# A graph-network kernel in which VectorE's running minimum is moved ahead of a step's first left-over columns

## The chip, the cores and the metric

One core of a Trainium2 chip runs the whole program. The metric is the device time of one execution in microseconds (us), lower being better.

## What is computed

The reference takes 6250 nodes with 64 features and 206250 edges sorted by destination, normalises the nodes, and runs four layers. In a layer each edge carries a message, and each node needs the sum, mean, variance, greatest and least of the messages that reach it; these feed a dense update with two batch norms.

```python
msg = jnp.concatenate([h[src], h[dst]], axis=1) @ WM + bM
s = jax.ops.segment_sum(msg, dst, num_segments=n)
mean_sq = jax.ops.segment_sum(msg * msg, dst, num_segments=n) / denom
mx = jnp.where(has, jax.ops.segment_max(msg, dst, num_segments=n), 0.0)
mn = jnp.where(has, jax.ops.segment_min(msg, dst, num_segments=n), 0.0)
agg = jnp.concatenate([mean, mx, mn, std, var, s], axis=1)
```

The part of a message that depends on the destination is added after the aggregation, so what is gathered or multiplied per edge is one row of a table of 6250 source nodes (the projected features and their squares).

## The kernel before

The kernel meets the segment sums and extremes in two ways at once, in what is called the dense phase of a layer below.

**One way is dense.** The 6250 destinations, in an order of their own, are cut into 13 chunks of 482 (`NCH`, `CH`); the sources into 50 blocks of 125 (`TILES`). For one edge per destination and block, TensorE multiplies the block's table (split in three bf16 parts) by a one-hot matrix. `products` (L1791) picks, for four blocks at a time, the source row of each destination into a pair of PSUM banks; a destination without an edge there gets a hugely negative number. `sums` (L1817) adds the rows of all blocks. In its middle it calls `flips` (L1800), which turns the hugely negative numbers in the same banks into hugely positive ones. VectorE folds the banks into running results: `greatest` (L1363, the first step of a chunk L1361) before the flip, `least_of` (L1374, the first L1372) after it. Three such pairs of banks are used in turn (`QRING`). A step is four blocks; a chunk has 13 steps, of which the last has two blocks, so a layer has 169 steps. TensorE's order in a step is products(i), first half of sums(i-1), flips(i-1), second half of sums(i-1). flips(i) waits for greatest(i), least_of(i) waits for flips(i), and products(i+3) waits for least_of(i).

**The other way is by columns.** Edges that are second, third and so on within one block for their destination are "left over". They are listed in 457 columns of 128 rows; GpSimd issues one indirect DMA for each (L883), which gathers 128 table rows into `rows`, and ScalarE masks what was gathered (L634). The columns come in 166 groups of one to three. VectorE treats a group twice, in `column_group`: part 0 folds greatest and least (L1435, L1436), part 1, six blocks later, adds the sums (L1440). The gathers go into a ring of five groups (`RING_G`): GpSimd may not issue the gathers of group g+5 before part 1 of group g has signalled `joined`.

**The order on VectorE** is written out. `columns_at` gives each half of a step (two blocks) the parts due there. Within step i VectorE runs greatest(i); in layer 0 also `compare` (L1399), which makes a one-hot matrix that later layers load instead; then the parts due in the first half; then least_of(i-1); then the parts due in the second half. By the code's own table 121 of a layer's 166 part 1s and 55 of its part 0s fall in the first half, 45 and 111 in the second.

**After the last part 1** GpSimd stores the column results (L875), and when they have landed gathers them back in node order by 50 indirect DMAs (L926). The node part of the layer, whose first VectorE instruction is L1575, waits for the first ten of those and for the dense results.

Of the kernel before, what the change touches and what calls it, by code (L numbers as in the profile page):

```python
# [119 lines left out]
def quad_of(at):  # L120

    return at // TILES * QUADS + at % TILES // QUAD
# [45 lines left out]
def build(nc, x, src, dst, WM, bM, WU, bU, gamma_t, beta_t, Wmix, bmix, gamma_o, beta_o, out):  # L168
# [15 lines left out]
    with ExitStack() as ctx:  # L184
# [205 lines left out]
        def wait(eng, s, value):  # L390

            wait_at(eng, s, value)
            if not isinstance(value, int):
                eng.sem_inc(S["passed"])

        def wait_at(eng, s, value):

            eng.wait_ge(S[s] if isinstance(s, str) else s, value)
# [13 lines left out]
        def group_at(g):  # L412

            done = sum(w for _, _, w in COL_GROUPS[0:g + 1])
            return COL_SPAN[0] + done * (COL_SPAN[1] - COL_SPAN[0]) // STATIC
# [514 lines left out]
        def _(dve):  # L930
# [263 lines left out]
            n = LIST // 2  # L1194
# [130 lines left out]
            def dense_part(l, numbers, chunks):  # L1325
# [3 lines left out]
                def parts(m):  # L1329


                    j0, n = batch_of(m)
                    t4 = T[0:NP, :, j0:j0 + n, :]
                    r4 = rest_r[0:NP, 0:n * 2 * P].rearrange("p (a j f) -> p a j f", a=2, j=n)
                    for some in ((0,), (1,)) if m == 0 else ((0, 1),):
                        wait(dve, "hi_done", finished(l, m) if some[-1] else l * (BATCHES + 1) + 1)
                        if m > 0 or some[0]:
                            wait(dve, "split_done", finished(l, m) - 1)
                        for a in some:
                            ins = nc.vector.tensor_tensor(r4[:, a], t4[:, a], spl(m)[:, a, :, 0, :], ALU.subtract)  # L1340
                        step(ins)
                        for a in some:
                            ins = nc.vector.tensor_copy(spl(m)[:, a, :, 1, :], r4[:, a])
                        step(ins)
                        for a in some:
                            ins = nc.vector.tensor_tensor(spl(m)[:, a, :, 2, :], r4[:, a], spl(m)[:, a, :, 1, :], ALU.subtract)  # L1346
                        ins.then_inc(S["split_done"], 1)

                def quad(i):

                    if i < QUADS - 1:
                        return QB[i % QRING], TOPS, LOWS
                    return PAIR[:, 0:CH], TOPS[:, 0, :], LOWS[:, 0, :]

                def greatest(n, i):

                    got, top, _ = quad(i)
                    wait_at(dve, "g_ready", n + i + 1)
                    wait_at(dve, "g_top", n + i + 1)
                    if i == 0:  # L1360
                        nc.vector.tensor_copy(top, got).then_inc(S["g_top"], 1)  # L1361
                    else:
                        nc.vector.tensor_tensor(top, top, got, ALU.max).then_inc(S["g_top"], 1)  # L1363

                def least_of(n, i):


                    got, _, low = quad(i)
                    wait_at(dve, "g_flip", n + i + 1)
                    wait_at(dve, "g_used", n + i + QRING + 1)  # L1370
                    if i == 0:
                        nc.vector.tensor_copy(low, got).then_inc(S["g_used"], 1)  # L1372
                    else:
                        nc.vector.tensor_tensor(low, low, got, ALU.min).then_inc(S["g_used"], 1)  # L1374
# [10 lines left out]
                def merge_halves(c):  # L1385

                    wait(dve, "crossed", l * NCH + c + 1)
                    nc.vector.tensor_tensor(stM[0:D, :], FX[0:D, :], stM[0:D, :], ALU.max)
                    nc.vector.tensor_tensor(stM[D:2 * D, :], FN[D:2 * D, :], stM[D:2 * D, :], ALU.min).then_inc(S["m_staged"], 1)

                def compare(g):


                    b = g % STREAM
                    dve.wait_ge(vb_ld[g % 2], 16 * (g // 2 + 1))
                    if g >= STREAM:
                        dve.wait_ge(S["dense_done"], g - STREAM + 2)
                        dve.wait_ge(oh_st[b], 16 * (g // STREAM))
                    nc.vector.tensor_scalar(BK[b], VB[g % 2], answers, None,  # L1399
                                            ALU.is_equal).then_inc(S["cmp"], 1)  # L1400
# [42 lines left out]
                def columns_at():  # L1443


                    due = {}
                    for g in range(NG):
                        k = group_at(g)
                        due.setdefault(k // 2, []).append((g, 0))
                        due.setdefault((k + SUM_LAG) // 2, []).append((g, 1))  # L1450
                    return due

                def dense(n0):

                    due = columns_at()
                    begin, end = COL_SPAN
                    opened = quad_of(min(group_at(g) for g in range(len(LEAD), NG)))
                    compared = [2]
                    if 0 in chunks:
                        n_step[0] = 0  # L1460
                        if numbers:
                            compare(0)
                            compare(1)
                        parts(0)
                    for c in chunks:
                        for i in range(QUADS):
                            at = c * TILES + QUAD * i
                            n = n0 + c * QUADS
                            if c == 0 and i % 2 == 0 and i // 2 + 1 < BATCHES:
                                parts(i // 2 + 1)  # L1470
                            if c * QUADS + i == quad_of(begin):
                                if numbers:
                                    dve.wait_ge(S["pos_ld"], 16)
                                    for o, v in ((1, first_r), (2, DEGr), (3, CNT)):
                                        nc.vector.tensor_copy(v[:, :], lists[:, :].rearrange("p (t f) -> p f t", f=PAY)[:, D + o, :]).then_inc(S["listed"], 1)
                                    dve.wait_ge(S["listed"], 3)
                                    for r in range(ROUNDS):
                                        ins = nc.vector.tensor_scalar(masks[:, FIRST[r]:FIRST[r + 1]], CNT[:, 0:WIDTH[r]], float(r), None, ALU.is_gt)
                                    ins.then_inc(S["listed"], 1)
                                wait(dve, "cleared", l * 3 + 3)  # L1480
                            if c * QUADS + i == opened:
                                wait(dve, "acc_ready", l * 3 + 3)
                            if i == 0 and (c or not numbers):
                                wait(dve, "folded", l * NCH + c)
                            greatest(n, i)
                            if numbers:
                                while compared[0] < NCH * GROUPS and compared[0] * RING <= at + 12:
                                    compare(compared[0])
                                    compared[0] += 1
                            for g, part in due.get(at // 2, []):  # L1490
                                column_group(g, part)
                            if i > 0:
                                least_of(n, i - 1)
                            if i < QUADS - 1:
                                for g, part in due.get(at // 2 + 1, []):
                                    column_group(g, part)
                            if i == 2 and c > 0:
                                merge_halves(c - 1)
                            if c * QUADS + i == quad_of(end + SUM_LAG) + 1:
                                with dve.If(rest > 0):  # L1500
                                    columns_past_the_plan()
                                with dve.If(more > 0):
                                    further_rounds(l)
                        least_of(n, QUADS - 1)
                        close_chunk(c)
                    if NCH - 1 in chunks:
                        merge_halves(NCH - 1)

                dense(0 if numbers else l * NQ)

            def node_part(l):
# [443 lines left out]
```

## Time and profile before

| what | us |
|---|---|
| median of three executions | 3894.86 |
| lowest and highest | 3887.85, 3898.64 |
| the profiled execution | 3899.44 |
| its span, first to last instruction | 3897.3 |
| dense phase of layer 0, and of layers 1 to 3 | about 376 to 1161, 1313 to 2002, 2165 to 2858, 3021 to 3720 |
| TensorE's granted clock, mean | 0.964 |

Times below are microseconds from the start of the span. The page of the profile gives an engine's busy time and its share of the span; a wait is put down to what ended it; an instruction's idle time before it stands in square brackets with its releaser.

### The profile page before, as it was taken

Reading aid. Unit: us, or ns where it says so; the run is one execution under the profiler, and the core shown is the slowest. Engines: PE = TensorE matmul, PEld = TensorE weight load, DVE = VectorE, ACT = ScalarE, POOL = GpSimd, SP = SyncE. Lnnn points to the kernel's source line nnn. Section 1 sums busy time; section 2 is a strip of 40 time slices with the busy share of each in tenths; the row PEclk is TensorE's granted clock in tenths of the full one; section 3 lists DMA queues with packets and bytes.
Section 4 is the critical chain, followed back from the end, with each engine's and each line's share of the span. In section 5 each row is a group of like instructions: output and inputs, shape, how many; then the busy total and the mean of one; then the engine's idle time right before and its main releaser. Section 6 shows DMA issues by size and latency. Waiting matters only on the chain.

```text
span 3897.3 us, 88696 instructions
## 1 busy us (share of the span) xinstructions
PE 3282.0 (84%) x29640; PEld 2057.8 (53%) x29640; DVE 3138.2 (81%) x6027; ACT 1169.8 (30%) x3428; POOL 2246.3 (58%) x2221
## 2 busy tenths in 40 slices
PE   0054599999989799999988799999987899999986
PEld 0022355455448566555667466565566465555575
DVE  6599589899878788888876788888876788888875
ACT  4302022222215322222225332222235222222243
POOL 6401577777753157777750177777750277777650
PEclk9997899999999899999999999999998999999998
DMA  7002678788882255555670356556660455566740
GB/s 213 17 0 75 223 262 274 267 280 285 292 296 92 92 168 175 185 178 182 205 242 15 120 177 184 171 182 196 205 206 4 146 185 171 177 188 193 224 155 34
DMA packets 237856, 675.58 MB, mean 173 GB/s; under 512 B 83074, under 2 KB 100310, under 8 KB 234758
## 3 DMA queue, kind: packets, MB, share of 16 engines
q1 hardware_dynamic: 126439, 426.27, 32.7%
q0 software_dynamic: 78400, 192.26, 17.1%
q10 hardware_dynamic: 32732, 54.15, 3.9%
q14 instruction: 215, 1.76, 0.1%
q8 instruction: 70, 1.15, 0.1%
HBM read 523.47 MB, written 153.60 MB: 174 GB/s over the span
## 4 chain that ended last, share of the span: by engine, by line
PE 25%; issue 20%; POOL 13%; DMA 12%; DVE 11%; ACT 2%; SPq 1%; DVEq 1%; ACTq 0%; POOLq 0%
POOL rows L883 12%; PE bank L1817 10%; DMA rows<-table,lists 9%; PE bank L1791 5%; PE bank L1884 4%; DVE accL L1440 2%; PE bank L1800 2%; DVE scr L1363 2%; DVE scr L1374 1%; SPq L478 1%; PE bank L1872 1%; DMA left<-accL 1%; DVE accL L1436 1%; POOL accL L926 1%; DMA RE<-ohd 1%
## 5 line engine op out<-in xcount | busy, mean ns | idle before, releaser
L883 POOL DMA_INDIRECT rows<-table,lists x1828 | 1854.1, 1014 | 760.7 <-issue 514.6
L1817 PE MATMUL bank<-RE,split 125*64 125x482 bf16 x15600 | 1833.1, 369 | 45.8 <-ACT scr L607 45.7
L1817 PEld LDWEIGHTS bank<-RE,split 125*64 125x64 bf16 x15600 | 948.0, 110 | 705.7 <-ACT scr L607 51.6
L634 ACT ACTIVATE split<-rows,masks 128x128 f32<-128x128 f32 x1828 | 602.3, 391 | 1658.9 <-DMA rows<-table,lists 1251.1
L1791 PE MATMUL bank<-RE,split 126*64 126x482 bf16 x7800 | 913.4, 369 | 40.7 <-DVE scr L1374 21.4
L1363 DVE TENSOR_TENSOR scr<-scr,bank 128x964 f32<-128x964 f32 x624 | 693.2, 1111 | 86.4 <-PE bank L1791 79.7
L1374 DVE TENSOR_TENSOR scr<-scr,bank 128x964 f32<-128x964 f32 x624 | 692.9, 1110 | 50.7 <-PE bank L1800 44.8
L1791 PEld LDWEIGHTS bank<-RE,split 126*64 126x64 bf16 x7800 | 470.4, 110 | 380.3 <-DVE scr L1374 38.0
L1800 PE MATMUL bank<-RE,flip_w 126*64 126x482 bf16 x2600 | 388.7, 371 | 83.8 <-DVE scr L1361 45.9
L1435 DVE TENSOR_TENSOR accL<-accL,rows 128x192 f32<-128x192 f32 (+2 forms) x664 | 225.5, 340 | 270.5 <-DMA rows<-table,lists 267.5
L1440 DVE TENSOR_TENSOR accL<-accL,split 128x384 f32<-128x384 f32 (+2 forms) x664 | 344.5, 519 | 1.7
L1800 PEld LDWEIGHTS bank<-RE,flip_w 126*64 126x64 bf16 x2600 | 152.7, 111 | 215.2 <-DVE scr L1361 62.7
L926 POOL DMA_INDIRECT accL<-left,nid x200 | 197.0, 985 | 104.5 <-issue 59.7
L1436 DVE TENSOR_TENSOR accL<-accL,rows 128x192 f32<-128x192 f32 (+2 forms) x664 | 222.5, 335 | 0.0
L866 POOL MEMSET accL<- 128x3328 f32 x4 | 11.5, 2871 | 328.8 <-DVE split L1346 327.8
L845 POOL DMA_INDIRECT pos_d<-accL,nid x50 | 55.4, 1107 | 231.5 <-DVE nid L1250 216.5
L1884 PE MATMUL bank<-W,rows 128*125 128x192 f32 x624 | 125.2, 338 | 41.6 <-ACT scr L763 41.6
L1399 DVE TENSOR_SCALAR RE<-RE,col 128x2410 bf16<-128x2410 bf16 x130 | 112.6, 867 | 25.1 <-DMA RE<-by_chunk 23.6
L1884 PE MATMUL bank<-W,RE 128*125 128x192 f32 x576 | 113.3, 333 | 19.4 <-ACT scr L763 15.6
L1884 PEld LDWEIGHTS bank<-W,rows 128*125 128x125 f32 x624 | 101.1, 192 | 49.7 <-issue 40.3
L1575 DVE TENSOR_TENSOR rows<-bank,accL 125x256 f32<-125x256 f32 x100 | 42.5, 425 | 81.9 <-PE bank L1860 69.4
L1884 PEld LDWEIGHTS bank<-W,RE 128*125 128x125 f32 x576 | 90.7, 187 | 27.5 <-issue 24.2
(282 smaller groups left out, 2750.4 us busy)
## 6 DMA issues: line engine op xcount, KB each, us to landing
RE<-ohd SPq DMA_DIRECT2D x395, 602.5 KB
RE<-by_chunk SPq DMA_DIRECT2D x130, 602.5 KB
ohd<-RE SPq DMA_DIRECT2D x130, 602.5 KB, 4.9
rows<-table,lists POOLq DMA_INDIRECT x1828
left<-accL POOLq DMA_DIRECT2D x20, 1280.0 KB, 7.4
dense_d<-scr ACTq DMA_DIRECT2D x104, 241.0 KB
split<-dense_d ACTq DMA_DIRECT2D x16, 625.0 KB, 6.5
table<-accL SPq DMA_DIRECT2D x36, 250.0 KB
```

Source lines behind the costliest of these rows:

```text
L634: ins = nc.scalar.activation(masked_rows[:, g % GM_RING * GC + k, :], ring[:, b * GC + k, :], ACT.Copy, scale=masks[:, m:m + 1])
L883: nc.gpsimd.indirect_dma_start(ring[:, b * GC + k, :], None, table, bass.IndirectOffsetOnAxis(ap=lists[:, c:c + 1], axis=0)).then_inc(col_ ...
L926: nc.gpsimd.indirect_dma_start(Lv[:, a, j, :], None, left, bass.IndirectOffsetOnAxis(ap=rank_i[:, i:i + 1], axis=0)).then_inc(l_ld[j // 5] ...
L1363: nc.vector.tensor_tensor(top, top, got, ALU.max).then_inc(S["g_top"], 1)
L1374: nc.vector.tensor_tensor(low, low, got, ALU.min).then_inc(S["g_used"], 1)
L1435: nc.vector.tensor_tensor(acc[:, :, 2 * D:3 * D], acc[:, :, 2 * D:3 * D], got[:, :, 0:D], ALU.max)
L1436: nc.vector.tensor_tensor(acc[:, :, 3 * D:4 * D], acc[:, :, 3 * D:4 * D], got[:, :, 0:D], ALU.min).then_inc(S["tops"], 1)
L1440: nc.vector.tensor_tensor(acc[:, :, 0:2 * D], acc[:, :, 0:2 * D], masked_rows[:, g % GM_RING * GC:g % GM_RING * GC + w, :], ALU.add).then_ ...
L1791: ins = nc.tensor.matmul(pair_bank(i, k)[half(k), 0:CH], split[0:NP + 1, k, q, 0:D], columns_of(k, NP + 1), start=q == 0, stop=q == 2)
L1800: ins = nc.tensor.matmul(pair_bank(i, k)[half(k), 0:CH], flip_w[0:NP + 1, :], columns_of(k, NP + 1), start=False, stop=True, skip_group_ch ...
L1817: ins = nc.tensor.matmul(SB[h * D:(h + 1) * D, 0:CH], split[0:NP, k, q, h * D:(h + 1) * D], columns_of(k, NP), start=k == 0 and q == 0, st ...
L1884: nc.tensor.matmul(u, aggT[j % 2][a][:, c * NP:(c + 1) * NP], W[:, W_U + c * 192:W_U + (c + 1) * 192], start=a == 0 and c == 0, stop=False ...
```

## The change

In the loop over steps in `dense`, the call of `least_of(n, i - 1)` moves ahead of the loop over the parts due in the first half of the step. All parts of a step now stand behind its minimum. Nothing is added or removed, and the orders of the other engines are the same.

```diff
@@ -1487,10 +1487,10 @@
                                 while compared[0] < NCH * GROUPS and compared[0] * RING <= at + 12:
                                     compare(compared[0])
                                     compared[0] += 1
+                            if i > 0:
+                                least_of(n, i - 1)
                             for g, part in due.get(at // 2, []):
                                 column_group(g, part)
-                            if i > 0:
-                                least_of(n, i - 1)
                             if i < QUADS - 1:
                                 for g, part in due.get(at // 2 + 1, []):
                                     column_group(g, part)
```

VectorE, at the step of layer 0 that holds the first part 1 of all (L1440). The names are line, operation, written and read tiles with the bank's number, and shape. Before:

```order
L1363 TENSOR_TENSOR scr<-scr,bank0 128x964
L1440 TENSOR_TENSOR accL<-accL,split 128x128
L1374 TENSOR_TENSOR scr<-scr,bank4 128x964
L1435 TENSOR_TENSOR accL<-accL,rows 128x3x64
L1436 TENSOR_TENSOR accL<-accL,rows 128x3x64
L1363 TENSOR_TENSOR scr<-scr,bank2 128x964
```

Now:

```order
L1363 TENSOR_TENSOR scr<-scr,bank0 128x964
L1374 TENSOR_TENSOR scr<-scr,bank4 128x964
L1440 TENSOR_TENSOR accL<-accL,split 128x128
L1435 TENSOR_TENSOR accL<-accL,rows 128x3x64
L1436 TENSOR_TENSOR accL<-accL,rows 128x3x64
L1363 TENSOR_TENSOR scr<-scr,bank2 128x964
```

The sum has moved behind one minimum; the part 0 of the second half, and the next greatest, stand where they stood.

VectorE, four steps later, where the first half holds a part 1 and a part 0. Before:

```order
L1363 TENSOR_TENSOR scr<-scr,bank0 128x964
L1399 TENSOR_SCALAR RE<-RE,col 128x2410
L1440 TENSOR_TENSOR accL<-accL,split 128x3x128
L1435 TENSOR_TENSOR accL<-accL,rows 128x3x64
L1436 TENSOR_TENSOR accL<-accL,rows 128x3x64
L1374 TENSOR_TENSOR scr<-scr,bank4 128x964
L1435 TENSOR_TENSOR accL<-accL,rows 128x64
L1436 TENSOR_TENSOR accL<-accL,rows 128x64
L1363 TENSOR_TENSOR scr<-scr,bank2 128x964
```

Now:

```order
L1363 TENSOR_TENSOR scr<-scr,bank0 128x964
L1399 TENSOR_SCALAR RE<-RE,col 128x2410
L1374 TENSOR_TENSOR scr<-scr,bank4 128x964
L1440 TENSOR_TENSOR accL<-accL,split 128x3x128
L1435 TENSOR_TENSOR accL<-accL,rows 128x3x64
L1436 TENSOR_TENSOR accL<-accL,rows 128x3x64
L1435 TENSOR_TENSOR accL<-accL,rows 128x64
L1436 TENSOR_TENSOR accL<-accL,rows 128x64
L1363 TENSOR_TENSOR scr<-scr,bank2 128x964
```

Here the minimum is ahead of both parts, and with them ahead of a possible wait for the gather that the first L1435 reads.

## Rows read from the trace of the kernel before

**Rows 1.** The page: busy us (share of the span) of each engine; granted clock.

```profile
PE 3282.0 (84%) x29640; PEld 2057.8 (53%) x29640; DVE 3138.2 (81%) x6027; ACT 1169.8 (30%) x3428; POOL 2246.3 (58%) x2221
...
PEclk9997899999999899999999999999998999999998
```

**Rows 2.** Stretches of layer 0 and layer 1: busy us (instructions), clock, DMA, GB/s.

```profile
800.00:900.00 100.00, 92.48 (x896) 50.59 (x894) 91.67 (x148) 26.73 (x77) 76.41 (x72) 1.00 0.83 273
1550.00:1650.00 100.00, 98.46 (x964) 56.77 (x962) 86.08 (x142) 28.82 (x83) 76.53 (x78) 1.00 0.57 178
```

**Rows 3.** GpSimd's waits, 540:1120, 1395:1960, 2245:2815, 3100:3670: us, times, longest.

```profile
POOL rows L883 <- DVE accL L1440: 22.3, 28, 3.1
...
POOL rows L883 <- DVE accL L1440: 17.7, 42, 2.5
...
POOL rows L883 <- DVE accL L1440: 13.1, 34, 2.5
...
POOL rows L883 <- DVE accL L1440: 51.0, 42, 35.7
```

**Rows 4.** VectorE's waits for gathers in 540:1120 and 1395:1960.

```profile
DVE accL L1435 <- DMA rows<-table,lists: 47.8, 42, 4.5
...
DVE accL L1435 <- DMA rows<-table,lists: 63.4, 60, 3.7
```

**Rows 5.** TensorE's waits for VectorE in layer 0, 540:1120.

```profile
PE bank L1800 <- DVE scr L1363: 25.0, 17, 4.2
...
PE bank L1791 <- DVE scr L1374: 8.3, 15, 2.6
```

**Rows 6.** GpSimd in order of time, layer 1: start, us, [idle before <-releaser].

```profile
1387.68 0.94 POOL L883 DMA_INDIRECT rows<-table,lists  x1 [29.75 <-DVE accL L1440]
...
1394.92 0.94 POOL L883 DMA_INDIRECT rows<-table,lists  x1 [2.53 <-DVE accL L1440]
...
1417.79 0.94 POOL L883 DMA_INDIRECT rows<-table,lists  x1 [0.30 <-issue]
```

**Rows 7.** VectorE and TensorE in order of time, layer 1, 1392:1396.

```profile
1392.51 1.16 DVE L1363 TENSOR_TENSOR scr<-scr,bank 128x964 f32<-128x964 f32 x1 [0.66 <-PE bank L1791]
1393.50 0.60 PE L1800 MATMUL bank<-RE,flip_w 126*64 126x482 bf16 x4
1393.58 0.55 DVE L1440 TENSOR_TENSOR accL<-accL,split 128x384 f32<-128x384 f32 x1
...
1394.22 1.16 DVE L1374 TENSOR_TENSOR scr<-scr,bank 128x964 f32<-128x964 f32 x1
...
1395.30 0.35 DVE L1435 TENSOR_TENSOR accL<-accL,rows 128x192 f32<-128x192 f32 x1
1395.57 0.35 DVE L1436 TENSOR_TENSOR accL<-accL,rows 128x192 f32<-128x192 f32 x1
```

**Rows 8.** VectorE in order of time, layer 1, 1612:1617.

```profile
1612.06 0.55 DVE L1440 TENSOR_TENSOR accL<-accL,split 128x384 f32<-128x384 f32 x1
1614.20 0.36 DVE L1435 TENSOR_TENSOR accL<-accL,rows 128x192 f32<-128x192 f32 x1 [1.60 <-DMA rows<-table,lists]
...
1614.75 1.15 DVE L1374 TENSOR_TENSOR scr<-scr,bank 128x964 f32<-128x964 f32 x1
1615.82 1.15 DVE L1363 TENSOR_TENSOR scr<-scr,bank 128x964 f32<-128x964 f32 x1
```

**Rows 9.** In order of time: last column parts of layers 0, 1, 2, store, node part.

```profile
1139.84 0.85 DVE L1399 TENSOR_SCALAR RE<-RE,col 128x2410 bf16<-128x2410 bf16 x1 [5.89 <-DMA RE<-by_chunk]
1140.60 0.42 DVE L1440 TENSOR_TENSOR accL<-accL,split 128x256 f32<-128x256 f32 x1
...
1980.60 0.58 POOL L875 DMA_DIRECT2D left<-accL  x1 [10.12 <-DVE accL L1440]
...
2008.03 0.42 DVE L1575 TENSOR_TENSOR rows<-bank,accL 125x256 f32<-125x256 f32 x1 [1.95 <-DMA accL<-left,nid]
...
2827.11 0.36 DVE L1435 TENSOR_TENSOR accL<-accL,rows 128x192 f32<-128x192 f32 x1 [2.40 <-DMA rows<-table,lists]
```

## The prediction

> **What bounds the kernel now.** I read the page first. TensorE is busy for 84% of the span and VectorE for 81% [rows 1]; each has stages of its own, so these shares alone say little. The busy time by stretch tells more. In the middle of layer 1 TensorE is busy 98.46 of 100 us, in layer 0 only 92.48, with VectorE at 91.67 [rows 2]. The granted clock is 1.00 in both, so the upper level (2.4 GHz) holds, and I count on no change there. GpSimd looks idle by a quarter, but between two gathers that wait for nothing it idles 0.30 us, as at 1417.79 [rows 6]. With that, layer 0 has 76.41 + 72 x 0.3 = 98.0 us of 100 filled, layer 1 76.53 + 78 x 0.3 = 99.9 [rows 2]. So three engines are nearly full at once, and the column stream on GpSimd has the least room.
>
> Then I read the waits. GpSimd waits for part 1 (L1440) in all four layers [rows 3]. Of each such wait 0.3 us is the gap that is there anyway, so what is real is 22.3 - 28 x 0.3 = 13.9 us in layer 0, 17.7 - 42 x 0.3 = 5.1 in layer 1, 2.9 in layer 2, and in layer 3, after the first wait of 35.7 is taken out, 51.0 - 35.7 - 41 x 0.3 = 3.0. In sum 24.9 us: this is all that a better order could take from the stream. VectorE in turn waits for gathers, 47.8 us in layer 0's stretch and 63.4 in layer 1's [rows 4]: it is ahead of the stream.
>
> Last I looked at who ends a layer. The node part's first instruction, L1575 at 2008.03, has idled 1.95 us for the gathers that follow the column store, which began at 1980.60, right behind the last part 1 [rows 9]. The dense side was ready earlier. L1575 waits for them in all four layers. So a last part 1 that is later by x makes the layer later by x.
>
> **The change, part by part.** The minimum takes 1.07 us from its start to the start of the next VectorE instruction (1614.75 to 1615.82, [rows 8]). It moves ahead of the first half's parts, 121 part 1s and 55 part 0s of 166 each by the code's table. TensorE, ScalarE, GpSimd and the DMA queues keep their orders. What moves in effect is (a) `joined` of 121 groups per layer, later by 1.07 us; (b) the minimum, earlier, which frees a bank pair for products three steps on; (c) the wait for a gather in a first half, which now has a minimum ahead of it; (d) the minimum's own wait for the flip, which the parts used to cover.
>
> *Start of the stream.* In each layer the first 13 gathers fill the ring, and the next waits until 1387.68 for the first part 1 [rows 6]. I matched each part to its half by counting: these first part 1s are all in first halves. So the stream starts 1.07 us later. In layers 1 to 3 the flip adds to it. At 1392.51 greatest starts as soon as TensorE's products allow, the part starts at 1393.58, and the flips end at 1393.50 + 0.60 = 1394.10 [rows 7]. The minimum in front would wait 0.52 us for them, so the part starts 1.07 + 0.52 = 1.6 us later, and with it the gather that now idles 2.53 us at 1394.92 [rows 6]. In layer 0 `compare` stands between and covers the flip: 1.07. Sum: 1.07 + 3 x 1.6 = **5.9 us**. Ends: 0 (absorbed later, where GpSimd waits anyway) and 5.9; I take the upper, since from 1417.79 on [rows 6] GpSimd issues nearly back to back to the end of the layer.
>
> *Inside the stream, layer 0.* Of the real waits for part 1, all but two have their part 1 in a first half. An upper end is each of the 28 [rows 3] by 1.07: 30 us. The lower end is 0, as a stream that is already late finds the next part done. I take less than half. The 28 waits fall into about 12 runs of neighbouring groups. A run moves as a whole, so it costs 1.07 once: 12.8 us. Against that stands (c): a gather that VectorE waits for in a first half no longer has the minimum behind it. At 1614.20 VectorE has idled 1.60 us and only then does the minimum [rows 8]; in the new order the minimum runs inside that idle time, the next greatest is 1.07 sooner, and the part 1 behind the next minimum comes when it came before. Nearly half of layer 0's waits for gathers are of this kind (19 of 43 by my count), and such a run costs nothing. **6 us**.
>
> *Inside the stream, layers 1 to 3.* Behind 1420 I find two, none and one wait of GpSimd that are real. 0 to 3.2 us; **2 us**.
>
> *End of the stream.* In layers 1 to 3 the last wait for a gather is in a first half and idles 2.40 us in layer 2 [rows 9]; it takes in one minimum, and the last part 1 gets one ahead of it: 0. In layer 0 the last part 1, at 1140.60, follows a compare that had waited 5.89 us [rows 9], and the minimum comes between: **1.1 us**.
>
> *Banks freed sooner, (b).* TensorE waits for the minimum 8.3 us in layer 0 [rows 5]. That is the most that (b) can give, and it is hidden as long as the column stream ends the layer: 0, lower end -8.3.
>
> *Gather against column work.* The gather at 1394.92 ran 0.94 us [rows 6] under L1435 and L1436 of 1395.30 and 1395.57 [rows 7], which is as short as any. The new order puts such parts where a minimum ran beside the first gather of a waiting group, so this row prices it at nothing. The Trainium skill ("SBUF — State Buffer", section "Who interferes with whom") has a rule against the change: a VectorE instruction with two SBUF inputs contends with a GpSimd instruction that reads SBUF, and the second of them blocks. By that rule each of some 50 waiting gathers could gain 0.35 us, 17 us more. The trace doesn't show it in this row.
>
> The sum is 5.9 + 6 + 2 + 0 + 0 + 1.1 = **15 us**. The profiled execution would go from 3899.4 to 3914.4 us; it lies 4.6 above the median of the runs, so for the median I take 3894.9 + 15 = **3910 us**.
>
> **The rivals.**
>
> *The ring absorbs it.* For this speaks that GpSimd's real waits are rare, 11 us in layers 1 to 3 together [rows 3], and that in those layers a part 1 in a first half is done some 4 us before its ring place is wanted (median of the gaps from L1440 to the gather). Then only the starts remain, in part: 0 to +8 us, 3899 us. Against it: the start moves the whole stream.
>
> *VectorE's idle time is filled, and it is faster.* The mechanism is (c). About 100 waits for gathers fall in first halves, and the first 1.07 us of each could be filled. TensorE waits 25.0 us for a late greatest in layer 0 [rows 5], and that would shrink. It decides if VectorE or TensorE, and not GpSimd, sets the pace of layer 0, where VectorE is at 91.67%. Against it: GpSimd has 13.9 us of real waits there, and the change lengthens those. If half the waits of layer 0 and the 8.3 us of (b) went: 7 + 8 = 15 us, 3880 us.
>
> *Every delay counts.* If no wait absorbs another: 5.9 + 30 + 3.2 + 1.1 = 40 us, 3935 us. With the port rule of the skill on top it would be 57 us, 3952; I give it 0.02.
>
> *The change doesn't do what it says.* Where VectorE is right behind TensorE, the minimum can't be earlier, since its flips aren't done [rows 7]; then parts are merely late. This is inside the forecast.
>
> **How the numbers follow.** Forecast (+6 to +28 us) 0.57; absorbed 0.20; faster 0.13; every delay counts 0.08; the port rule 0.02. A measurement of this kernel tells some 0.3%, 11.7 us, from no change. Of the forecast about 0.37 lies above that and 0.20 below. So slower is 0.37 + 0.08 + 0.02 = 0.47, the same 0.20 + 0.20 = 0.40, faster 0.13. The range reaches down into the faster case, to 3886, and up to the case in which every delay counts, 3936. The forecast's own range is 3901 to 3923.
>
> **What would show it.** The first gather behind the ring's fill comes 1.1 us later against its L1440's greatest, and the idle time that stands at 1394.92 grows by about 1.6 us. GpSimd's waits for L1440 grow, in layer 0 most, by 5 us or more. L1374 waits for L1800 more often than the 9 times or so of a layer now. VectorE's wait for gathers in first halves shrinks, in second halves it grows. L1575 still waits for the gathers behind the column store, and each layer is longer, layers 1 to 3 by 2 to 3 us, layer 0 by some 8. I am wrong if GpSimd's waits don't grow, if L1575 stops waiting for those gathers, or if TensorE's waits in layer 0 fall by more than the stream loses.

## The result, and the profile after

The changed kernel takes 3917.25 us (median of five, 3910.29 to 3919.79) against 3894.65 beside it on the same chip (3887.85 to 3898.64). The ratio is 1.0058, with a 95% interval of 1.0046 to 1.0069: it is **22.6 us slower**. (The ratio is not that of the two medians; in the experiments below the two differ by up to 0.0017.) The profiled execution took 3919.79 us, its span 3917.8.

The page of the kernel after, to be laid beside [rows 1]. In a group's row stand busy us and the mean ns of one, then the idle time before it and its releasers.

```profile
PE 3296.2 (84%) x29640; PEld 2047.1 (52%) x29640; DVE 3137.4 (80%) x6027; ACT 1169.7 (30%) x3428; POOL 2267.2 (58%) x2221
...
L883 POOL DMA_INDIRECT rows<-table,lists x1828 | 1872.9, 1025 | 766.6 <-issue 510.4
```

VectorE's work is what it was. GpSimd is busy 2267.2 us, up from 2246.3 [rows 1]: 20.9 us more for the same 2221 instructions, about the size of the loss. In the page of before, L883 had 1854.1 us and a mean of 1014 ns; so 18.8 of the 20.9 us are gathers whose issue lasts longer. A DMA issue that lasts longer is not what I had looked for.

Where in the program? L1575 of layer 0, first and last start of its 25, in the kernel before and after:

```profile
L1575 DVE TENSOR_TENSOR rows<-bank,accL x25: 424/425/426, 1169.1 to 1268.7; 125x256 f32<-125x256 f32 x25
```

```profile
L1575 DVE TENSOR_TENSOR rows<-bank,accL x25: 424/425/426, 1188.1 to 1287.9; 125x256 f32<-125x256 f32 x25
```

19.0 us later, and the end of the span is 20.5 later. From the first L1791 to the first L1575, layer 0 takes 793.1 us before and 812.5 after; layers 1 to 3 together take 2098.8 and 2098.0. **All of the loss lies in layer 0.** The groups of GpSimd's gathers in layer 0 (450:1180), before and after:

```profile
L883 POOL DMA_INDIRECT rows<-table,lists x457 | 490.2, 1073 | 180.0 <-issue 132.0 <-DVE accL L1440 41.2 <-DMA table<-accL 6.9
```

```profile
L883 POOL DMA_INDIRECT rows<-table,lists x457 | 511.3, 1119 | 182.1 <-issue 124.1 <-DVE accL L1440 51.5 <-DMA table<-accL 6.4
```

Busy +21.1 us, idle +2.1. The middle of layer 0 shows what is left for the others, against [rows 2]:

```profile
800.00:900.00 100.00, 89.85 (x836) 46.49 (x834) 86.11 (x141) 24.56 (x71) 74.89 (x67) 0.98 0.75 255
1550.00:1650.00 100.00, 95.87 (x940) 53.80 (x936) 83.78 (x138) 27.44 (x81) 75.54 (x77) 1.00 0.55 173
```

GpSimd issues 67 times in 100 us where it was 72, and VectorE is down from 91.67 to 86.11. The granted clock is 0.98 where it was 1.00, and 0.97 against 0.99 over 540:1120. The loss doesn't need that: gather_waits_min (below) loses 19 us with 0.99 there. The waits of 540:1120, against [rows 3 to 5]:

```profile
DVE accL L1435 <- DMA rows<-table,lists: 74.5, 47, 5.2
...
PE bank L1800 <- DVE scr L1363: 49.5, 35, 4.6
...
POOL rows L883 <- DVE accL L1440: 28.8, 49, 3.1
...
PE bank L1791 <- DVE scr L1374: 0.6, 2, 0.4
```

VectorE waits for gathers 74.5 us, not 47.8; TensorE waits for a late greatest 49.5 us, not 25.0; the 8.3 us for the minimum are gone. GpSimd's waits for part 1 are 49 where there were 28, but less the 0.3 us gap they are 28.8 - 14.7 = 14.1 us, against 13.9 before. The stream isn't starved; it is slow in itself.

**What makes a gather's issue last.** VectorE and GpSimd of the kernel before, in order of time (start, us):

```profile
618.72 0.94 DVE L1399 TENSOR_SCALAR RE<-RE,col 128x2410 bf16<-128x2410 bf16 x1
619.58 0.54 DVE L1440 TENSOR_TENSOR accL<-accL,split 128x384 f32<-128x384 f32 x1
620.04 1.15 DVE L1374 TENSOR_TENSOR scr<-scr,bank 128x964 f32<-128x964 f32 x1
```

```profile
619.36 1.11 POOL L883 DMA_INDIRECT rows<-table,lists  x1 [0.30 <-issue]
620.77 0.94 POOL L883 DMA_INDIRECT rows<-table,lists  x1 [0.30 <-issue]
```

The gather of 619.36 begins under compare (L1399) and lasts 1.11 us; the next begins under the minimum (L1374) and lasts 0.94, the usual value. After:

```profile
617.48 1.15 DVE L1374 TENSOR_TENSOR scr<-scr,bank 128x964 f32<-128x964 f32 x1
618.55 0.55 DVE L1440 TENSOR_TENSOR accL<-accL,split 128x384 f32<-128x384 f32 x1
...
619.55 1.15 DVE L1363 TENSOR_TENSOR scr<-scr,bank 128x964 f32<-128x964 f32 x1
...
634.83 0.85 DVE L1399 TENSOR_SCALAR RE<-RE,col 128x2410 bf16<-128x2410 bf16 x1
635.59 1.15 DVE L1374 TENSOR_TENSOR scr<-scr,bank 128x964 f32<-128x964 f32 x1
636.65 0.42 DVE L1440 TENSOR_TENSOR accL<-accL,split 128x256 f32<-128x256 f32 x1
```

```profile
618.69 1.23 POOL L883 DMA_INDIRECT rows<-table,lists  x1 [0.30 <-issue]
...
634.96 1.52 POOL L883 DMA_INDIRECT rows<-table,lists  x1 [0.31 <-issue]
636.79 1.64 POOL L883 DMA_INDIRECT rows<-table,lists  x1 [0.30 <-issue]
```

618.69 begins under a sum (L1440) and lasts 0.29 us too long. 634.96 begins under compare and lasts 0.58 too long, about what compare still had to run (635.59 - 634.96 = 0.63). So a held gather looks as if its 0.94 us began only when the VectorE instruction is done. The next, 1.83 us later, begins under the sum behind the minimum and is held again.

I laid the start of every gather of layer 0 against the VectorE instruction that ran at that moment, in classes: none; one that reads PSUM (greatest and minimum); compare; one that reads two tiles of SBUF (L1435, L1436, L1440 and the ends of chunks). Count, and sum of the time over 0.945 us:

| | none | PSUM | compare | two from SBUF |
|---|---|---|---|---|
| before | 65, 0.9 us | 213, 3.8 us | 93, 38.3 us | 86, 15.4 us |
| after | 77, 0.3 us | 149, 10.1 us | 77, 30.7 us | **154, 38.4 us** |

In layers 1 to 3 of the kernel before, 929 gathers that begin under nothing or under a PSUM reader are as short as any (mean excess -1 ns), and 435 that begin under two inputs from SBUF have 69.2 us over, 159 ns each. The 10.1 us under PSUM readers in layer 0 are gathers that began less than 0.5 us ahead of compare; such a gather lasts longer by about the time from its start to compare's. So what counts is what runs when the issue begins, and a compare right behind. In layer 0 of the new order 68 more gathers begin under column work. What the new order moves is itself a little less than the code's table says: in the trace of before, 114 part 1s and 52 part 0s of a layer stand between a greatest and its minimum; 7 and 3 more of the table's 121 and 55 lie in the first step of a chunk, which has no minimum to move.

### The profile page after: what moved, and what is told of

Its sections match the earlier page's. It is cut to its first block, busy times and chain, and to the rows that moved or that the text cites. A ratio compares the mean times of both kernels' runs of the same rounds, so it can differ in the third digit from the quotient of the medians.

```text
span 3917.8 us, 88696 instructions
## 1 busy us (share of the span) xinstructions
PE 3296.2 (84%) x29640; PEld 2047.1 (52%) x29640; DVE 3137.4 (80%) x6027; ACT 1169.7 (30%) x3428; POOL 2267.2 (58%) x2221
## 3 DMA queue, kind: packets, MB, share of 16 engines
q0 software_dynamic: 78400, 192.26, 16.3%
## 4 chain that ended last, share of the span: by engine, by line
PE 26%; issue 22%; POOL 17%; DVE 16%; DMA 13%; ACT 3%; ACTq 2%; SPq 1%; DVEq 1%; POOLq 0%
POOL rows L883 14%; PE bank L1817 10%; DMA rows<-table,lists 10%; PE bank L1791 5%; PE bank L1884 3%; DVE scr L1374 2%; PE bank L1800 2%; DVE accL L1440 2%; ACTq L691 1%; POOL accL L839 1%; DVE scr L1363 1%; SPq L478 1%; PE bank L1872 1%; DMA left<-accL 1%; DVE RE L1169 1%
## 5 line engine op out<-in xcount | busy, mean ns | idle before, releaser
L883 POOL DMA_INDIRECT rows<-table,lists x1828 | 1872.9, 1025 | 766.6 <-issue 510.4
L1791 PE MATMUL bank<-RE,split 126*64 126x482 bf16 x7800 | 915.0, 370 | 20.7 <-DMA RE<-ohd 9.6
L1374 DVE TENSOR_TENSOR scr<-scr,bank 128x964 f32<-128x964 f32 x624 | 693.1, 1111 | 76.4 <-PE bank L1800 74.4
L1791 PEld LDWEIGHTS bank<-RE,split 126*64 126x64 bf16 x7800 | 468.9, 110 | 364.4 <-issue 33.7
L1800 PE MATMUL bank<-RE,flip_w 126*64 126x482 bf16 x2600 | 389.7, 372 | 107.6 <-DVE scr L1363 84.4
L1435 DVE TENSOR_TENSOR accL<-accL,rows 128x192 f32<-128x192 f32 (+2 forms) x664 | 226.7, 341 | 308.9 <-DMA rows<-table,lists 304.5
L1440 DVE TENSOR_TENSOR accL<-accL,split 128x384 f32<-128x384 f32 (+2 forms) x664 | 344.8, 519 | 2.5
L1800 PEld LDWEIGHTS bank<-RE,flip_w 126*64 126x64 bf16 x2600 | 148.1, 111 | 250.5 <-DVE scr L1363 126.3
L1436 DVE TENSOR_TENSOR accL<-accL,rows 128x192 f32<-128x192 f32 (+2 forms) x664 | 222.9, 336 | 0.0
L1884 PEld LDWEIGHTS bank<-W,rows 128*125 128x125 f32 x624 | 100.9, 191 | 50.3 <-issue 40.6
L1399 DVE TENSOR_SCALAR RE<-RE,col 128x2410 bf16<-128x2410 bf16 x130 | 110.7, 852 | 17.5 <-DMA RE<-by_chunk 15.8
L1575 DVE TENSOR_TENSOR rows<-bank,accL 125x256 f32<-125x256 f32 x100 | 42.5, 425 | 83.4 <-PE bank L1860 70.5
```

What stands on the lines that cost most here:

```text
L883: nc.gpsimd.indirect_dma_start(ring[:, b * GC + k, :], None, table, bass.IndirectOffsetOnAxis(ap=lists[:, c:c + 1], axis=0)).then_inc(col_ ...
L1435: nc.vector.tensor_tensor(acc[:, :, 2 * D:3 * D], acc[:, :, 2 * D:3 * D], got[:, :, 0:D], ALU.max)
L1436: nc.vector.tensor_tensor(acc[:, :, 3 * D:4 * D], acc[:, :, 3 * D:4 * D], got[:, :, 0:D], ALU.min).then_inc(S["tops"], 1)
L1440: nc.vector.tensor_tensor(acc[:, :, 0:2 * D], acc[:, :, 0:2 * D], masked_rows[:, g % GM_RING * GC:g % GM_RING * GC + w, :], ALU.add).then_ ...
L1791: ins = nc.tensor.matmul(pair_bank(i, k)[half(k), 0:CH], split[0:NP + 1, k, q, 0:D], columns_of(k, NP + 1), start=q == 0, stop=q == 2)
L1800: ins = nc.tensor.matmul(pair_bank(i, k)[half(k), 0:CH], flip_w[0:NP + 1, :], columns_of(k, NP + 1), start=False, stop=True, skip_group_ch ...
```

## The experiments

For each kernel I divide layer 0 in the same way. *Held* is the sum of its gathers' time over 0.945 us, *waits* GpSimd's idle time between them over 0.31 us, both from the 14th gather on; *dense* runs from the first L1791 to the first L1575. The ratio is to the kernel before on the same chip, all runs timed.

| kernel | held | waits | sum | dense, layer 0 | ratio (95%) |
|---|---|---|---|---|---|
| before | 58.8 | 18.9 | 77.7 | 793.1 | 1 |
| after | 79.6 | 21.3 | 100.9 | 812.5 | 1.0058 (1.0046, 1.0069) |
| layer0_only | 78.0 | 19.8 | 97.8 | 809.3 | 1.0048 (1.0032, 1.0063) |
| layers123_only | 55.0 | 16.3 | 71.3 | 785.4 | 1.0000 (0.9986, 1.0014) |
| part0_behind | 63.0 | 12.7 | 75.7 | 786.3 | 0.9982 (0.9966, 0.9999) |
| min_then_compare | 45.9 | 22.9 | 68.8 | 781.8 | 1.0007 (0.9991, 1.0023) |
| late_compare | 75.3 | 8.7 | 84.0 | 794.9 | 1.0002 (0.9986, 1.0019) |
| gather_waits_min | 50.1 | 39.8 | 89.9 | 800.9 | 1.0052 (1.0033, 1.0070) |
| lag4_old | 80.8 | 6.3 | 87.1 | 797.3 | 1.0012 (0.9999, 1.0024) |
| lag4_new | 78.6 | 5.8 | 84.4 | 797.8 | 1.0020 (1.0005, 1.0036) |
| lag4_part0_behind | 77.5 | 4.7 | 82.2 | 790.4 | 0.9987 (0.9975, 0.9999) |
| one_input_old | 32.6 | 21.3 | 53.9 | 764.7 | 0.9859 (0.9834, 0.9884) |
| one_input_new | 33.6 | 36.3 | 69.9 | 780.4 | 0.9868 (0.9845, 0.9891) |
| one_input_lag4_new | 29.2 | 11.0 | 40.2 | 750.6 | 0.9798 (0.9767, 0.9828) |

The column "sum" goes with layer 0's time almost one to one over 60 us, while neither of its two parts does. That is bookkeeping, not yet a cause: what is left, the start, 443 gathers at 1.25 us and the tail, stays at 708 to 715 us in all fourteen kernels. It shows that whatever an order costs comes through the gather stream. All holds and waits are of one profiled execution each. Layer 0 of before and of layers123_only is the same program and differs by 7.7 us: that much a single profile scatters.

### In which layers

```diff
+                            if i > 0 and numbers:
+                                least_of(n, i - 1)
                             for g, part in due.get(at // 2, []):
                                 column_group(g, part)
-                            if i > 0:
+                            if i > 0 and not (numbers):
                                 least_of(n, i - 1)
```

`numbers` is true in layer 0; the second kernel has `not numbers`.

> The minimum moves ahead in layer 0 alone; layers 1 to 3 keep the order of before. Theory 1 (locked issue: a gather whose issue begins while VectorE runs an instruction with two SBUF inputs, or compare, is held until that ends, and the new order in layer 0 puts more gathers there): +17 to +22 us against before, nearly the whole difference of the change. Theory 2 (late sums: GpSimd gets its ring places one minimum later, the theory of the prediction): +6 to +10 us, the rest being in layers 1 to 3.

> The minimum moves ahead in layers 1 to 3 alone. Theory 1: -2 to +4 us against before, since the number and the length of gathers that begin under column work did not change there. Theory 2: +7 to +10 us, three starts of 1.6 us and a few waits.

3909.1 us (+20.8) and 3887.15 (-1.2) against 3888.33, as theory 1 had it. The change costs what it costs in layer 0, and in layers 1 to 3 nothing. In 450:1180, layer0_only shows the gathers' loss, layers123_only doesn't:

```profile
L883 POOL DMA_INDIRECT rows<-table,lists x457 | 509.7, 1115 | 179.2 <-issue 121.7 <-DVE accL L1440 51.6 <-DMA table<-accL 5.9
```

```profile
L883 POOL DMA_INDIRECT rows<-table,lists x457 | 486.4, 1064 | 176.9 <-issue 131.2 <-DVE accL L1440 39.0 <-DMA table<-accL 6.8
```

### Only part 0 behind the minimum

```diff
                             for g, part in due.get(at // 2, []):
-                                column_group(g, part)
+                                if part == 1:
+                                    column_group(g, part)
                             if i > 0:
                                 least_of(n, i - 1)
+                            for g, part in due.get(at // 2, []):
+                                if part == 0:
+                                    column_group(g, part)
```

> In all layers the part 1s of a step's first half stay ahead of the minimum as before, and only its part 0s go behind it. No sum is late, and a first half's wait for a gather is filled by the minimum. Theory 2: faster than before by 5 to 15 us. Theory 1: between -5 and +10 us, because the part 0s now touch the second half's parts and gathers that begin there are held longer.

3888.08 us, ratio 0.9982. Sums in their old place: no loss. The folds (L1435, L1436) moved alone cost nothing; the price needs the moved sums (L1440).

### Another place for compare

min_then_compare is the new order with the minimum ahead of compare too; late_compare runs part 1s, minimum, compare, part 0s.

```diff
                             greatest(n, i)
+                            if i > 0:
+                                least_of(n, i - 1)
                             if numbers:
...
                             for g, part in due.get(at // 2, []):
                                 column_group(g, part)
-                            if i > 0:
-                                least_of(n, i - 1)
```

> Like the changed kernel, but in layer 0 the minimum also stands ahead of compare, so that compare and all parts of a step touch. The sums come when they come in the changed kernel. Theory 2: within 3 us of the changed kernel, +20 to +25 us against before. Theory 1: the instructions that hold a gather's issue stand in one piece, a held gather waits longer: another +8 to +20 us, so +30 to +42 us against before, with the mean of L883 in layer 0 above 1130 ns (before 1073, changed 1119).

> First half's part 1s, minimum, compare, first half's part 0s, second half's parts. The sums of the first half now come ahead of compare, 0.8 us sooner than before in layer 0; compare is followed by column work. Theory 2: faster than before by 5 to 15 us. Theory 1: by the gathers held (mean of L883 in layer 0 between 1040 and 1120 ns), -12 to +10 us.

min_then_compare took 3889.65 us, as long as before, which neither theory had expected: its sums are as late as in the changed kernel, and its gathers are held for less.

```profile
L883 POOL DMA_INDIRECT rows<-table,lists x457 | 477.3, 1044 | 185.3 <-issue 131.7 <-DVE accL L1440 45.9 <-DMA table<-accL 7.7
```

That led to a count of what a gather meets that follows, without a wait, one that began under compare. The held one is let go when compare ends, and the next begins about 1.25 us later. Before, a sum (0.47 us) and the minimum (1.07) follow compare, and 46 of 74 such gathers begin under a PSUM reader. After, the minimum comes first, and 64 of 70 begin under column work, where most are held a second time. In min_then_compare it is 30 of 52. I take it from this that the order decides where the beat of the gathers falls against VectorE's. late_compare (3890.11 us) holds them nearly as long as the changed kernel (75.3 us), but its sums are early and the waits fall to 8.7: no change in time (theory 1 had allowed that, theory 2 not).

### No two inputs from SBUF

```diff
-                        nc.vector.tensor_tensor(acc[:, :, 2 * D:3 * D], acc[:, :, 2 * D:3 * D], got[:, :, 0:D], ALU.max)
+                        nc.vector.tensor_reduce(acc[:, :, 2 * D:3 * D], got[:, :, 0:D].unsqueeze(3), AX.X, ALU.max)
```

L1436 and L1440 likewise, in the old order and the new. The three instructions last nearly as long as before (0.54 to 0.55 us for the wide L1440) but read one tile; the columns' results are not accumulated.

> The order of before. The three column instructions (L1435, L1436, L1440) become reductions over one element, which read only what was gathered and not the running result: one SBUF input in place of two, same number of elements. So the columns' greatest, least and sums are not accumulated and the output isn't the reference's. Theory 1: a gather is no longer held by column work, so in layer 0 the 86 gathers that began under it lose 15 us, and in layers 1 to 3 the 20 to 25 us per layer that gathers are held vanish; TensorE is full there, so little of it reaches the end. Faster than before by 15 to 40 us, and L883's mean in layers 1 to 3 goes from 994 to 950 ns. Theory 2: no change beyond 5 us.

> The same reductions with one input, in the order of the changed kernel. Theory 1: the difference between the two orders, 19 to 22 us, shrinks to within 6 us of the one-input kernel in the old order, since what it came from is gone. Theory 2: the sums are as late as in the changed kernel, so this is slower than the one-input kernel in the old order by 15 us or more.

3825.37 and 3832.05 us against 3883.32. VectorE is busy 7.6 us less (3130.6, not 3138.2), GpSimd issues as many gathers, and the old order is 58 us faster, more than either theory had said (15 to 40). In its trace the holds of all four layers fall by 72 us, from 126.6 to 54.5. So the holds under column work are nearly all of what the kernel before paid here; the new order gains more, 1.0058 to 0.9868. Rows of the pages, old and new order:

```profile
L883 POOL DMA_INDIRECT rows<-table,lists x1828 | 1782.0, 975 | 754.2 <-issue 511.8
```

```profile
L883 POOL DMA_INDIRECT rows<-table,lists x1828 | 1777.3, 972 | 784.7 <-issue 504.7
```

What is held in layer 0 is now the same in both orders (32.6 and 33.6 us, most of it by compare, some 5 by the ends of chunks; in layers 1 to 3 it is 5 to 8 us a layer). In the medians the price of the new order falls from 22.6 to 6.7 us, and the intervals overlap; theory 1 had said within 6, theory 2 at least 15. The two profiled executions, the fastest of four and the slowest of four, lie 24.6 us apart, of which 15.7 are in layer 0, as waits (21.3 and 36.3). So a second cause is left, the late sums, and how large it is four runs each don't tell.

### Late sums alone, and early sums

gather_waits_min keeps VectorE's old order; GpSimd also waits, before it reuses a place of the ring, for the minimum that follows the part 1 which frees it.

```diff
                     wait(pool, "joined", l * NG + g + 1)
+                    half = (group_at(g - RING_G) + SUM_LAG) // 2 if g >= RING_G else 0
+                    c, i = half // 25, half % 25 // 2
+                    if g >= RING_G and half % 25 % 2 == 0 and i > 0:
+                        wait(pool, "g_used", l * NQ + c * QUADS + i + QRING + 1)
```

> VectorE keeps the order of before in all layers. Only GpSimd's gathers are made as late as in the changed kernel: where a group's ring place is freed by a part 1 in a first half, they also wait for the minimum behind it. Theory 2: most of the change's difference, +12 to +22 us against before. Theory 1: small, 0 to +8 us: 1 to 2 us of wait more in layers 1 to 3 and some 3 to 5 in layer 0, and the 31 gathers of layer 0 that began right under a minimum now begin under what follows it.

3902.7 us, ratio 1.0052: a ring place that comes free one minimum later is enough for 19 us, without a change on VectorE, as theory 2 had it (12 to 22) and theory 1 had not (0 to 8). In 540:1120 (here the gather is L887 and the minimum L1378):

```profile
POOL rows L887 <- DVE scr L1378: 33.8, 40, 3.8
POOL rows L887 <- DVE accL L1444: 17.5, 26, 2.2
```

The gathers are held for 8.7 us less than before and wait for 20.9 more. A gather that has waited begins elsewhere, and one that was held needs no longer wait: the two stand in for each other, and only their sum reaches the end.

The other side gives the ring its slack back: part 1 comes four blocks behind its part 0, not six, from block 104 on.

```diff
-                        due.setdefault((k + SUM_LAG) // 2, []).append((g, 1))
+                        due.setdefault((k + (4 if k >= 104 else SUM_LAG)) // 2, []).append((g, 1))
```

> The changed order, but from block 104 of each layer on a group's part 1 comes four blocks after its part 0 instead of six, so ring places come free about 2 us sooner than in the changed kernel, sooner than in the kernel before too. Theory 2 (late sums cost the time): the loss is gone, between -10 and +3 us against before, with GpSimd's waits for L1440 in layer 0 below 10 us. Theory 1 (held issues cost it): the gathers of layer 0 are still held as often where column work stands in one block, +10 to +25 us against before.

> The order of before with the same shorter lag. Theory 2: ring waits in layer 0 (13.9 us) go, faster than before by 5 to 15 us. Theory 1: what is held decides; more part 1s now stand in second halves beside part 0s, -8 to +8 us. The difference to the changed order with the short lag is above 12 us by theory 1, below 6 us by theory 2.

> The short lag, with only the first half's part 0s behind the minimum: no sum is late and waits for gathers are filled. A candidate for a faster kernel. Both theories: no slower than the old order with the short lag; theory 2: -10 to -20 us against before, theory 1: -10 to +5 us.

3898.18, 3893.68 and 3888.2 us against 3888.05. With early sums the two orders differ by 4.5 us, not 22.6, and their intervals overlap: that is theory 2's "below 6". That neither of the first two is faster than before is theory 1's. GpSimd's row of 540:1120, new order and old:

```profile
POOL rows L883 <- DVE accL L1440: 14.9, 49, 0.3
```

```profile
POOL rows L883 <- DVE accL L1440: 13.3, 38, 1.1
```

49 x 0.3 = 14.7: no real wait is left in the new order. But the holds stay, and in the old order they rise from 58.8 to 80.8 us: gathers that no longer wait run on into column work.

### Both taken away

The new order, one input, and early sums.

> The minimum ahead of all columns, the three column operations with one input as in the kernel with one input and the new order (their results are not accumulated), and part 1 four blocks behind part 0 from block 104 on. If the new order costs time in layer 0 by two things alone, gathers held behind column work and sums that come too late for the ring, then with both taken away it should be at least as fast as one input in the old order: ratio to before 0.983 to 0.987 (against 0.9859), and in layer 0 the gathers' waits fall from 36 us to about 6 while the time held stays near 33 us, so the stream from the 14th gather on falls from 626 to about 600 us. If a sum four blocks behind its part 0 brings a cost of its own, as the pair with two inputs suggests (held 80.8 us in the old order against 58.8), the holds grow to 50 us or more and the ratio stays at 0.987 or above.

3812.55 us against 3894.0, ratio 0.9798 (0.9767, 0.9828): faster than one input in the old order, whose interval begins above it (at 0.9834), and than the 0.983 to 0.987 expected. The gathers' waits are 11.0 us, and with one input the early sums bring no holds (29.2 us):

```profile
L883 POOL DMA_INDIRECT rows<-table,lists x457 | 460.8, 1008 | 171.6 <-issue 120.4 <-DVE accL L1440 44.9 <-DMA table<-accL 6.3
```

Nothing of the new order's price is seen any more with both taken away. One input with early sums in the old order was not run, so how much of the last 0.6% is the lag's own gain stays open.

## Why the prediction was right and where it was wrong

The forecast was slower by 15 us, and it is slower by 22.6, inside the range and inside the forecast's own (3901 to 3923). The direction came from the right thought, that the column stream has the least room and sums that come later hurt it. The split was wrong: I had 8.2 us in layer 0 and 6.8 in layers 1 to 3, and the traces show 19.4 and -0.8. That the total came near is partly luck.

*Gather against column work, priced at 0: this step failed.* It measured +20.8 us of holds in layer 0 (58.8 to 79.6). I took the price from one row, the gather at 1394.92 [rows 6], over L1435 and L1436 [rows 7]. But that gather **began** under the minimum of 1394.22 (it ran to 1395.38); what followed didn't touch it. One row that begins in one class says nothing of the other. The rule that I had weighed and given 0.02 is right in kind: the Trainium skill ("SBUF — State Buffer", section "Who interferes with whom") says that a VectorE instruction with two SBUF inputs contends with a GpSimd instruction that reads SBUF, and that the second to issue blocks. The traces agree for a gather that comes second: 0 ns under PSUM readers, 159 ns on average under two inputs, and nearly nothing left with one input. By that rule I had reckoned 17 us more; the holds grew by 20.8. The traces don't show a VectorE instruction that comes second blocked: a wide L1440 that starts while a gather is being issued lasts 550 ns on average, one that starts beside none 555 (396 and 168 of them, kernel before). In the same section the Trainium skill infers that a tensor_tensor doesn't stall descriptor generation, since that needs the write interface; here the issue of an indirect DMA was held by it.

That the holds were the larger cause is not shown by this. Layer 0's sum of holds and waits grew by 23.2 us, 20.8 of them held. With one input 16.0 of them stay (69.9 against 53.9), now as waits; with early sums none do (84.4 against 87.1; each of these is one profile, and they scatter by some 8 us); and late sums alone cost 19 us. On the other side stand the medians with one input, only 6.7 us apart. So the moved sums are needed for the loss (min_then_compare shows that they don't bring it in every order), and it shows as holds; how it divides between the two stays open.

*Inside the stream, layer 0, 6 us.* The waits grew by 2.4 us (18.9 to 21.3), in 540:1120 by 0.2; my sign had been 5 us or more. As a cause late sums are real, and alone they cost 19 us over all layers (gather_waits_min), where I had put 6 and 2; but here holds took the place of waits. Part0_behind adds that without moved sums there is no loss.

*Start of the stream, 5.9 us.* From a layer's first L1791 to its 14th gather it took 0.2 us longer in layer 0 (112.9, 113.1) and 1.9 in layers 1 to 3 together (233.6, 235.5), so 2.1. In layer 1, against [rows 6, 7]:

```profile
1408.21 0.94 POOL L883 DMA_INDIRECT rows<-table,lists  x1 [30.64 <-DVE accL L1440]
...
1416.34 0.95 POOL L883 DMA_INDIRECT rows<-table,lists  x1 [3.13 <-DVE accL L1440]
```

```profile
1412.21 1.16 DVE L1363 TENSOR_TENSOR scr<-scr,bank 128x964 f32<-128x964 f32 x1 [0.19 <-PE bank L1791]
1413.93 1.16 DVE L1374 TENSOR_TENSOR scr<-scr,bank 128x964 f32<-128x964 f32 x1 [0.56 <-PE bank L1800]
1415.00 0.55 DVE L1440 TENSOR_TENSOR accL<-accL,split 128x384 f32<-128x384 f32 x1
```

The minimum does wait 0.56 us for the flips, as reckoned (0.52). But the idle time grew from 2.53 to 3.13 us, by 0.6 and not 1.6, as the greatest starts 4.00 us behind the first gather where it started 4.83 behind (1392.51 - 1387.68). I take it that TensorE got its banks sooner, which no run singles out. What was late didn't reach the end of a layer.

*Inside the stream, layers 1 to 3, 2 us.* Nothing: 2098.8 and 2098.0 us, and 1.0000 for layers123_only. I had expected 2 to 3 us for each. L1374 waits for L1800 26 times in 1395:1960 against some 9, as I had said, and it costs nothing:

```profile
DVE accL L1435 <- DMA rows<-table,lists: 71.2, 68, 3.6
...
DVE scr L1374 <- PE bank L1800: 13.2, 26, 0.9
```

*End of the stream, 1.1 us.* From the last gather of layer 0 to L1575 it took 42.0 us, not 45.9: no sign of it.

*Banks freed sooner, 0.* TensorE's wait for the minimum fell from 8.3 to 0.6 us, hidden as I had said; its wait for the greatest rose by 24.5.

*Rivals.* The ring absorbs it: true of layers 1 to 3. VectorE's idle time is filled: its waits for gathers did fall in first halves of layer 0 (20.2 to 17.3 us, by my matching) and rose in second halves (30.5 to 64.6), as expected, but it is the stream that sets the pace. The sum of 15 was near for a partly wrong reason: starts at 5.9 us that cost 2.1 and didn't reach a layer's end, and nothing for the holds, in which most of the loss shows.

## What to carry to other kernels

When GpSimd issues DMAs in a tight stream, look at the duration of the issue itself and at what VectorE runs when each begins; a mean of 1014 ns against a median of 944 is a cost that no wait shows. To price a collision, sort all such pairs by what runs at the start, not by one row where they overlap. A small reordering can move a regular stream onto another engine's beat: judge it by holds plus waits together, since each takes the other's place.

## What was not expected of the hardware

- An indirect DMA of 128 rows takes GpSimd 0.944 us to issue. If it begins while VectorE runs an instruction with two SBUF inputs, or compare (bf16 tensor_scalar), it lasts longer by about what that one still has to run, mostly 0.05 to 0.6 us. Where further such instructions stand right behind, some gathers are held through those too (23 of 118 in layer 0 of the kernel before) and some not; which is open. The longest there begins under compare and is held through L1440, L1435 and L1436 as well, 1.58 us:

```profile
854.69 2.53 POOL L883 DMA_INDIRECT rows<-table,lists  x1 [0.30 <-issue]
```

- Under greatest and minimum, with one input in PSUM, the excess is 0 unless compare follows.
- A two-input instruction that starts after the gather has begun doesn't slow it (1394.92 [rows 6] is one of many), be it only 0.05 us after. A compare that starts 0.02 to 0.48 us after does: of 34 such gathers of layer 0 after, each lasts longer by that interval and some 20 ns. Why the two differ is open.
- The holds under column work cost the kernel before about 1.4% (58 us). A form whose running results don't lie in SBUF with the gathered rows might save it; that was not tried. No kernel that computes the whole beats the one before clearly: part0_behind (0.9966 to 0.9999) and lag4_part0_behind (0.9975 to 0.9999) are at the edge of what can be told.
